# A fused attention kernel: one PSUM buffer for a weight product, two evacuations exchanged between ScalarE and VectorE

## What is computed

```python
xn = layernorm(x)
Q = xn @ W1 + b1; K = xn @ W2 + b2; V = xn @ W3 + b3
attn = softmax(Q @ K.T / 32) @ V @ W4 + b4
W_real = unfold(G1_R, G2_R); W_imag = unfold(G1_I, G2_I)      # 512 x 512 each
x_real, x_imag = split(xn, 2)
ffn = concat(x_real @ W_real.T - x_imag @ W_imag.T + bias_real,
             x_real @ W_imag.T + x_imag @ W_real.T + bias_imag)
out = x + attn + ffn
```

## Time and profile before

| | |
|---|---|
| median of 2 timed runs | 1699.01 us (1697.82 to 1700.19) |
| the profiled execution | 1700.31 us |
| its span on the slowest core (5) | 1698.8 us |
| spans of the eight cores | 1693.2 to 1698.8 us |
| busy: TensorE, VectorE, ScalarE, GpSimd | 1554.7, 756.4, 482.9, 128.7 us |

### The profile page before, as it was taken

One profiled execution on the slowest core, in us unless ns is written; L12 is line 12 of the kernel. 1 busy time (PEld: TensorE's weight loads), 2 busy tenths in 40 slices (PEclk: granted clock), 3 DMA queues, 4 the chain that ended last, 5 costly groups with the idle time before them and its releaser, 6 DMA issues.

```text
span 1698.8 us, 25404 instructions; the slowest of 8 cores (1693.2 to 1698.8 us)
## 1 busy us (share of the span) xinstructions
PE 1554.7 (92%) x8496; PEld 764.5 (45%) x8496; DVE 756.4 (45%) x1863; ACT 482.9 (28%) x873; POOL 128.7 (8%) x107
## 2 busy tenths in 40 slices
PE   1668899998999999999999999999999999999998
PEld 1423565655444444444444444444444444444443
DVE  3212333333455445535553555355445535553544
ACT  0101333333322323322333222322322222332322
POOL 2000111112000000000000000000000000000000
PEclk9669999999999999999999999999999999999999
DMA  9234121213211101111111110111101111110001
GB/s 185 39 62 63 51 75 53 73 59 101 77 38 50 38 26 62 38 38 38 38 38 37 38 50 26 50 38 41 47 26 60 41 38 38 38 38 26 26 26 38
DMA packets 69531, 83.48 MB, mean 49 GB/s; under 512 B 39699, under 2 KB 49947, under 8 KB 69406
## 3 DMA queue, kind: packets, MB, share of 16 engines
q1 hardware_dynamic: 56030, 42.01, 8.7%
q10 hardware_dynamic: 9216, 33.56, 6.2%
q0 software_dynamic: 4160, 6.29, 2.5%
HBM read 69.27 MB, written 18.87 MB: 52 GB/s over the span
## 4 chain that ended last, share of the span: by engine, by line
PE 87%; DVE 4%; SPq 3%; DMA 3%; issue 2%; ACT 0%; DVEq 0%; POOL 0%; ACTq 0%; POOLq 0%
PE po L559 13%; PE po L660 13%; PE po L664 13%; PE sp_a L559 7%; PE sp_b L559 7%; PE pf L589 3%; PE sp_a L424 3%; PE sp_a L526 3%; PE sp_b L526 3%; PE sp_b L424 3%; PE pf L448 3%; PE po L448 3%; PE ptA L631 2%; PE ptB L631 2%; SPq L284 2%
## 5 line engine op out<-in xcount | busy, mean ns | idle before, releaser
L664 PE MATMUL po<-V,ETs 128*128 128x512 bf16 x1024 | 388.0, 379 | 0.0
L660 PE MATMUL po<-V,ETs 128*128 128x512 bf16 x1024 | 388.0, 379 | 0.0
L559 PE MATMUL po<-KT,QXT 128*128 128x512 bf16 x1024 | 231.4, 379 | 0.0
L619 DVE TENSOR_REDUCE r<-Et 128x1 f32<-128x512 bf16 x256 | 173.6, 678 | 32.1 <-ACT Et L615 31.4
L380 POOL TENSOR_SCALAR xnn<-xg,rstd,nmr 128x1024 bf16<-128x1024 f32 x64 | 76.6, 1202 | 1250.9 <-DVE nmr L376 1250.9
L615 ACT ACTIVATE Et<-Ssb,ngm 128x512 bf16<-128x512 f32 x256 | 165.0, 711 | 12.6 <-PE ptB L631 11.3
L572 ACT ACTIVATE Ssb<-sp_a 128x512 f32<-128x512 f32 x64 | 38.3, 598 | 419.0 <-DVE mx L564 301.4
L559 PEld LDWEIGHTS po<-KT,QXT 128*128 128x128 bf16 x1024 | 100.2, 98 | 120.8
L564 DVE TENSOR_REDUCE mx<-po 128x1 f32<-128x512 f32 x128 | 88.5, 692 | 131.4 <-PE po L559 131.4
L664 PEld LDWEIGHTS po<-V,ETs 128*128 128x128 bf16 x1024 | 100.0, 98 | 94.4
L660 PEld LDWEIGHTS po<-V,ETs 128*128 128x128 bf16 x1024 | 99.9, 98 | 94.5
(11 more groups left out here) (95 smaller groups left out, 1784.9 us busy)
## 6 DMA issues: line engine op xcount, KB each, us to landing
xg<-x ACTq DMA_DIRECT2D x64, 512.0 KB, 3.7
xr<-x SPq DMA_DIRECT2D x32, 512.0 KB, 3.6
out<-xr SPq DMA_DIRECT2D x32, 512.0 KB, 2.6
KT<-W POOLq DMA_DIRECT2D x2, 2048.0 KB, 46.5
Ssb<-W SPq DMA_DIRECT2D x8, 512.0 KB, 6.8
Wproj<-W POOLq DMA_DIRECT2D x1, 2048.0 KB, 23.7
scr<-V SPq DMA_DIRECT2D x2, 1024.0 KB, 6.7
V<-scr SPq DMA_DIRECT2D x64, 32.0 KB, 3.0
```

The lines of the kernel that those rows point to most:

```text
L559: P.add("tensor", lambda e, tb=tb, c=c, si=si, spv=spv: e.matmul(spv, QT[:, c, si * 128:(si + 1) * 128], KT[:, c, tb * 512:(tb + 1) * 512] ...
L619: P.add("vector", lambda e, tb=tb: e.reduce_sum(r8[:, tb:tb + 1], Et[:, tb % 4, :], axis=AX.X), waits=[("exp", i, tb)] + ([("rr", i - 1)] ...
L660: P.add("tensor", lambda e, tb=tb, q=q, tj=tj: e.matmul(po[:, 0:512], ETs[:, tb % 4, q, :], V0[:, tj, 0:512], start=(tj == 0), stop=(tj == ...
L664: P.add("tensor", lambda e, tb=tb, q=q, tj=tj: e.matmul(po[:, 512:1024], ETs[:, tb % 4, q, :], V0[:, tj, 512:1024], start=(tj == 0), stop= ...
```

## The change

Three edits. (A) The eight blocks of W3p all go into `po`; block m waits for the evacuation of block m-1, and the bias matmuls, which still use `pf`, no longer wait for an evacuation. (B) The copies of the transposed tiles out of `ptA` and `ptB` (L404) go from VectorE to ScalarE, as an Identity activation. (C) The copies of the score blocks to `Ssb` (L572) go from ScalarE to VectorE.

```diff
@@ W3p, in emit_pro_tail @@
-            pv = po if m % 2 == 0 else pf
-                        pv[:, h * 512:(h + 1) * 512], W3T[:, k, m * 128:(m + 1) * 128],
+                        po[:, h * 512:(h + 1) * 512], W3T[:, k, m * 128:(m + 1) * 128],
...
-                               ("W3pe", m - 2) if m > 1 else None],
+                               ("W3pe", m - 1) if m > 0 else None],
...
-                W3p[:, m, :], pv[:, :], AF.Identity),
+                W3p[:, m, :], po[:, :], AF.Identity),
...
-        free["po"] = ("W3pe", 6)
-        free["pf"] = ("W3pe", 7)
+        free["po"] = ("W3pe", 7)
@@ emit_ln_tps @@
-            P.add("vector", lambda e, u=u, c0=c0, bank=bank: e.tensor_copy(
-                xnT[:, u, c0:c0 + 2, :], bank[:, :, :]),
+            P.add("scalar", lambda e, u=u, c0=c0, bank=bank: e.activation(
+                xnT[:, u, c0:c0 + 2, :], bank[:, :, :], AF.Identity),
@@ score blocks @@
-                P.add("scalar", lambda e, tb=tb, spv=spv: e.activation(
-                    Ssb[:, tb * 512:(tb + 1) * 512], spv, AF.Identity),
+                P.add("vector", lambda e, tb=tb, spv=spv: e.tensor_copy(
+                    Ssb[:, tb * 512:(tb + 1) * 512], spv),
```

More of the change, by code:

```diff
@@ L296, in emit_pro_tail @@
         for m in range(8):
-            pv = po if m % 2 == 0 else pf
             for h in range(2):
                 for k in range(8):
-                    P.add("tensor", lambda e, m=m, h=h, k=k, pv=pv: e.matmul(
-                        pv[:, h * 512:(h + 1) * 512], W3T[:, k, m * 128:(m + 1) * 128],
+                    P.add("tensor", lambda e, m=m, h=h, k=k: e.matmul(
+                        po[:, h * 512:(h + 1) * 512], W3T[:, k, m * 128:(m + 1) * 128],
                         W4b[:, k, h * 512:(h + 1) * 512],
@@ L304, in emit_pro_tail @@
                         waits=[("w3te", 31), ("LW4",),
-                               ("W3pe", m - 2) if m > 1 else None],
+                               ("W3pe", m - 1) if m > 0 else None],
                         mark=("W3pm", m, h) if k == 7 else None)
-            P.add("scalar", lambda e, m=m, pv=pv: e.activation(
-                W3p[:, m, :], pv[:, :], AF.Identity),
+            P.add("scalar", lambda e, m=m: e.activation(
+                W3p[:, m, :], po[:, :], AF.Identity),
                 waits=[("W3pm", m, 0), ("W3pm", m, 1)], mark=("W3pe", m))
-        free["po"] = ("W3pe", 6)
-        free["pf"] = ("W3pe", 7)
+        free["po"] = ("W3pe", 7)
         W3PDONE = ("W3pe", 7)
```

## The result

| | before | after |
|---|---|---|
| median of the runs | 1699.69 us (10 runs) | 1781.15 us (11 runs) |
| the profiled execution | 1700.31 us | 1767.02 us |
| its span on the slowest core (5) | 1698.8 us | 1765.0 us |
| spans of the eight cores | 1693.2 to 1698.8 us | 1753.2 to 1765.0 us |

The account below looks back on a forecast made before the run. TensorE, 87% of the chain that ended last, was taken as the bound, so only its waits count. 6.2 + 15.2 + 28.6 = 50.0 us took the profiled 1700.3 to 1750.3, about 1749 as median; range 1730 to 1771.

Parts of the forecast that it names:

- A + B up to group 1: Prologue to group 1: the next tiles' load, issued behind the eight copies, comes 5.8 later, slower rounds add 0.4; 6.2 us.
- stage 1 passes: Stage 1 transposes: first copy 0.79 later behind V's evacuation, plus slower bank rounds; 1.17 per pass, 13 times, 15.2 us.
- stage 2 tiles: Stage 2: TensorE idles 1.02 us per tile because exp 6 stands behind four copies; 28 times, 28.6 us.
- C: Score copies on VectorE: 1.48 us a block under TensorE's 1.73, and F covers the later exp; cost 0.
- those loads: Stage 1 loads issued behind the copies arrive about 2.8 later; costed at nothing, up to 7 us if room is gone.
- the cover of A: W3p: seven waits of 1.44 us, 10.1, mostly hidden by TensorE's wait at V of tile 1; A itself costs about 0.2.
- the exps held behind the copies: Stage 2: exps 6 and 7 wait behind four copies; block 6's transposes start at 737.12 instead of 736.02.
- the late first copy of a pass: Stage 1: V's evacuation precedes the copies on ScalarE, so the first copy comes at +1.18, 0.79 later.
- rival 1: W3p: gaps of 1.44 us keep the clock at its lower level; 7 x 2.8 = 19.6, giving 1769; chance 8%.
- Rival 3: L404: TensorE's 44.3 us of waits are a busy VectorE's queue and go; 1661, faster; chance 3%.
- rival 4: Stage 2 scores: VectorE's score copy takes 1.20 and binds above 0.93; 38 us, giving 1787; chance 5%.
- Rival 2: Stage 2: block 6 need not wait for exp 6, leaving 5 us there, total 26, 1726; chance 8%, including loss half hidden.

Follow-up runs that it names:

- e_c: Kernel before with only the score copies moved to VectorE (edit C); ratio 1.0012 against the kernel before.
- e_both: Changed kernel with exps 6 and 7 ahead of the copies and useless matmuls in stage 1's stalls; 1727.2 to 1731.0 us, 1.0146 against the kernel before.
- e_a: Kernel before with only the `po` edit, one buffer for W3p (edit A); ratio 0.9994 against the kernel before.
- e_exps: Changed kernel with exps 6 and 7 emitted ahead of the copies in stage 2's 28 tiles; 1739.5 to 1740.7 us, 1.0225 against the kernel before.
- e_fill: Changed kernel with useless 512-column matmuls in the stalls of stage 1's passes; 1756.7 to 1758.8 us, 1.0324 against the kernel before.
- e_vlate: Changed kernel with V's second-tile evacuation put behind the eight copies on ScalarE in 13 passes; 1752.9 to 1755.2 us, 1.0304 against the kernel before.

## Why the prediction was wrong

| step | predicted | measured | from |
|---|---|---|---|
| A + B up to group 1 | 6.2 | 3.5 | start of W3p to first K of group 1, timeline |
| stage 1 passes | 13 x 1.17 = 15.2 | 13 x 1.10 = 14.3 | 4.00 against 2.90 |
| stage 2 tiles | 28 x 1.02 = 28.6 | 28 x 0.97 = 27.2 | first transposes to the next matmuls, 2.91 against 1.94 |
| C | 0 | 2 (0 to 4) | `e_c`; the tiles of the profile show 0.8 |
| clock, stage 1 | 0 | 7 x 1.55 = 10.9 | 8.66 against 7.11 for K |
| clock, stage 2 (core 5) | 0 | 6 x 1.67 = 10.0 | 3.40 against 1.73 for 8 matmuls |

With 0.8 for C the measured column gives 66.7 for 66.2. What stands in no row cancels: W3p starts 1.7 earlier (110.30 against 112.00), K of group 1 is 0.3 shorter and the stretch from the last pass to Q 0.5, and against these K loses 2.5 behind the issue of the loads (13 x 0.11 and once 1.07). The forecast had looked at those loads and put them at nothing. The other cores have shorter spans (1753.2 to 1762.1).

The direction and all the mechanisms of the sum held: the order on ScalarE, the cover of A, the exps held behind the copies, the late first copy of a pass. The two copies came out within 0.02 us and the two stalls within 0.1.

*The step that failed* is the one that costs TensorE's idle time at its length alone. It stands in rival 1: "By that rule the same gaps of stage 1 and 2 would cost too; the trace shows none of it there so far." What the trace of before showed were passes of 2.90 us with gaps of 0.43; I had worked out first gaps about three times as long in both stages and still read the old rows as evidence for them. The sum had no term for the clock in either stage, and the runs show one of 10.9 + 10.0 = 21 us out of the 66. The rule of the Trainium skill ("TensorE: Matmul & The Clock Gate", section "A second HAM failure mode: psum-queue depth-cycling") was weighed at W3p, where this trace does not bear it out (seven stalls of 1.44, clock full), and not at the places where it does (0.54 behind a pass). `e_both`, which has no falls and no stall on exp, is within 0.4 us of what the other terms come to.

*Rival 1* as priced is refuted: at W3p the clock stayed full. *Rival 3* and *rival 4* are refuted by the waits. *Rival 2* is refuted too, but its price was sound: with the exps ahead a tile costs 0.24 more than before, where 0.2 was worked out.

*A slip without effect*: 9 ns more for each copy, as weighed beside the sum, would add 1.3 us and not 2, since the forecast itself puts 86 ns (0.39 to 0.476) at 12 us.

*A and B around the prologue* was 2.7 too large. The load is issued 5.6 later against W3p's start (167.96 - 110.30 against 164.03 - 112.00; predicted 5.8), but from the issue to the first statistic are now 3.5 us, where it was 5.7. The transfer was quicker; no run here isolates why.

*What stays open.* Why only about half the passes of stage 1 and some tiles of stage 2 have the fall, different ones on each core, and why the pass of `e_a` has one that the same pass of the kernel before has not; no run tells. And the slower group of the changed kernel, which sets its median and puts the time outside the range: in those runs exactly two cores, of one neighbouring pair, have 1779 to 1782 us at a mean clock of 0.952 to 0.957, the other six 1751 to 1766 at some 0.97. Some ten more falls on those two cores would make it (an estimate, 16 us over 1.67), but no profile of such a run was taken. With the stage 2 stall taken out (`e_exps`) the four runs agree within 1.2 us, but those of `e_fill`, which keeps that stall, agree within 2.1, so this says little.

## What to carry to other kernels

An evacuation that is moved to another engine takes over that engine's order: ask what stands in front of it and what now stands behind it, since the busy time of ScalarE here fell (482.9 to 415.2 us) while the kernel lost 4%. Price a new stall of TensorE at its length, and then ask what the clock does behind it; the old trace is evidence only where it has gaps as long as the new ones. And a stall that waits for an evacuation is often best removed by order alone: transposes in the middle of independent matmuls gave 3.4% with the same instructions.

## What the runs showed of the hardware

Whether the clock falls depends on more than the longest gap. At W3p, 1.44 us without a matmul start between 3.45 us of dense ones left it full seven times. In stage 1, 1.32 + 0.46 + 0.45 us of idle time in a pass of 4.00 with only short transposes between them brought it down behind 6 or 7 of 13 passes; 0.51 + 0.46 + 0.46 in 3.19 behind 2 or 3 (`e_vlate`); 0.24 three times in 3.98, the rest filled with matmuls of 512 columns (`e_fill`), not at all. Some 0.43 three times in 2.90 to 3.04 did not in the kernel before, but in `e_a` once on each of three cores. In stage 2, 0.51 + 1.24 in 2.91 did so at 2 to 6 of 28 tiles; 0.51 and 0.35 there, with the exps ahead, at none. More work in the stalls made the kernel faster by 9 to 11 us.

An Identity activation of 256 bf16 columns out of PSUM takes 0.385 us on ScalarE, where VectorE's copy takes 0.29; of 512 fp32 columns VectorE's copy takes 0.692 and ScalarE's 0.598. The Trainium skill, "ScalarE: Activation LUTs", section "What ACT_TABLE_LOAD costs", gives 399 ns for the first, an estimate by its formula for an ACTIVATE with immediate scale and bias; the trace has 385.
